# Two groups on the two partition halves with paired 64-row products, a sparse diagonal of the maxima, and GpSimd's style product first in its slot

## The reference

```python
styles = w @ (affine_w * gain).T + affine_b                       # one style per batch
y = clip(einsum(x * styles, weight) * dcoefs + bias, -256, 256)   # modulated linear
Q, K, V = X @ Wq, X @ Wk, X @ Wv          # X = y; 16 heads in 4 groups, key width 64
attn = softmax(Q K.T / 8)                 # 128 x 128 for each head
x = x + y + (attn @ V) @ Wpost
kx = modulated_linear(x)                  # 16 heads of 8 channels within one token
out = modulated_linear(softmax(kx kx.T / sqrt(8)) kx)
x = x + experts(out)                      # 8 experts, top 2, capacity rule
```

## Time and profile before

| | |
|---|---|
| Median of three runs | 663.79 us (662.43 to 665.09) |
| Profiled execution, own time | 664.89 us |
| Its span, first to last instruction | 663.1 us |
| TensorE, VectorE, ScalarE, GpSimd busy | 96%, 79%, 62%, 43% of the span |
| Mean granted clock of TensorE | 0.989 of full |

### The profile page before, as it was taken

One profiled execution on the slowest core, in us unless ns is written; L12 is line 12 of the kernel. 1 busy time (PEld: TensorE's weight loads), 2 busy tenths in 40 slices (PEclk: granted clock), 3 DMA queues, 4 the chain that ended last, 5 costly groups with the idle time before them and its releaser, 6 DMA issues. The chain is left out here.

```text
span 663.1 us, 15299 instructions
## 1 busy us (share of the span) xinstructions
PE 634.1 (96%) x4420; PEld 511.7 (77%) x4420; DVE 521.7 (79%) x1155; ACT 414.1 (62%) x823; POOL 288.1 (43%) x251
## 2 busy tenths in 40 slices
PE   8899999999999999999999999999999996899998
PEld 8687778787878787878787877778787786756765
DVE  6246888888888888888888888888888879767776
ACT  2776677767676777777777777777767531434443
POOL 5122555555555555555555555555555466000000
PEclk9999999999999999999999999999999997899999
DMA  7200000000000000000000000000000000000004
GB/s 245 47 1 1 1 2 1 0 0 0 0 0 0 0 0 0 0 0 0 0 0 0 0 0 0 0 0 0 0 0 1 2 1 1 0 0 0 1 0 127
DMA packets 9363, 7.18 MB, mean 11 GB/s; under 512 B 1088, under 2 KB 8832, under 8 KB 9216
## 3 DMA queue, kind: packets, MB, share of 16 engines
q1 hardware_dynamic: 9344, 6.94, 3.6%
HBM read 4.84 MB, written 2.10 MB: 10 GB/s over the span
## 5 line engine op out<-in xcount | busy, mean ns | idle before, releaser
L1087 POOL TENSOR_TENSOR pair<-kx 128x1152 f32<-128x1152 f32 x32 | 82.4, 2574 | 164.2 <-ACT kx L831 159.9
L611 PEld LDWEIGHTS bank_a<-v,prob 128*128 128x128 f32 x1024 | 127.0, 192 | 17.0 <-issue 15.8
L611 PE MATMUL bank_a<-v,prob 128*128 128x65 f32 x1024 | 131.8, 272 | 0.0
L603 PE MATMUL bank_t<-qT,k_one 128*128 128x512 f32 x256 | 130.7, 592 | 0.0
L295 DVE TENSOR_REDUCE row_max<-bank_s 128x4 f32<-128x512 f32 x128 | 87.3, 682 | 13.2 <-PE bank_s L594 8.9
L831 ACT ACTIVATE prob<-bank_t 128x512 f32<-128x512 f32 x128 | 76.4, 597 | 29.5 <-PE bank_t L603 26.5
L440 DVE CAST k<-k_one 64x512 bf16<-64x512 f32 x32 | 50.2, 1568 | 54.5 <-ACT k_one L831 54.5
L1067 POOL TENSOR_TENSOR mix_hi<-mix_hi 128x512 f32<-128x512 f32 (+2 forms) x96 | 80.2, 835 | 7.5
L1079 POOL TENSOR_TENSOR neg_diag<-neg_max,own_w 16x512 bf16<-16x512 f32 x32 | 36.3, 1135 | 96.2 <-ACT neg_max L831 83.5
L831 ACT ACTIVATE qT<-misc 64x512 f32<-64x512 f32 x128 | 75.6, 591 | 3.9 <-PE misc L618 1.6
L618 PEld LDWEIGHTS misc<-yT,wq_sb 128*128 128x128 f32 x512 | 64.5, 192 | 15.9 <-issue 14.9
(11 more groups left out here) (155 smaller groups left out, 1127.1 us busy)
## 6 DMA issues: line engine op xcount, KB each, us to landing
out<-acc_all SPq DMA_DIRECT2D x8, 256.0 KB, 2.3
x_all<-in_xT SPq DMA_DIRECT2D x1, 1024.0 KB, 9.6
w_sb<-in_w SPq DMA_DIRECT2D x2, 512.0 KB
x_all<-in_xT SPq DMA_DIRECT2D x1, 768.0 KB, 7.4
wq_sb<-in_wq SPq DMA_DIRECT2D x1, 512.0 KB, 6.1
wpost_sb<-in_wpost SPq DMA_DIRECT2D x1, 512.0 KB, 9.6
x_all<-in_xT SPq DMA_DIRECT2D x1, 256.0 KB, 3.1
b_rows<-in_b SPq DMA_DIRECT2D x16, 4.0 KB
```

The source lines that it names most:

```text
L603: mm(bank_t[g % 2][:, :, :], k_one[:, j, g, :], qT[:, j, HPG * g:HPG * (g + 1), :], start=False, stop=True).then_inc(s_t_mm, 1)
L611: last = mm(att_bank(g)[:, w, :], prob[:, g % 2, w, :], v1[:, j, g, :], start=(w == 0), stop=True, skip_group_check=True)
L1087: G.tensor_tensor(pair[:, :, :], bass.AP(kx2, jc * 2 * P, [[4 * P, P], [0, SHIFTS], [1, P]]), bass.AP(kx2, jc * 2 * P, [[4 * P, P], [MD, S ...
```

## The change

- `qT`, `q16`, `kT` and `k16` hold two groups at once: an even group on partitions 0 to 63, an odd one on 64 to 127. The columns of `wq` are put in another order on the host for it. `copy_q` is one copy of 128 partitions for each bank, `narrow_q` has half the columns, and the memsets of the unused halves go.
- `scores_t` takes a pair of groups: two bfloat16 products of 64 rows into `bank_t0` and `bank_t1`, then four float32 products of 64 rows and 256 columns that alternate between the halves.
- `row_max` becomes a bfloat16 tile of four blocks of 128 columns, in which only the places of a diagonal are written. Four small products with `ident16` into `bank_s` turn it, and one ScalarE copy with scale -1 makes `neg_diag`. GpSimd's instruction and `neg_max` go.
- `k16` and `v1` are made by ScalarE out of PSUM; VectorE's L440 goes.
- The order in a slot changes on each engine. In TensorE's, the second half of the queries comes before the maxima's product, `attend` 0 and 1 follow each other, and the style product of the batch after next stands in the middle and not at the end. VectorE makes `yT` after the first two groups. GpSimd makes `xs` first.

The core of the diff:

```diff
-                V.tensor_reduce(row_max[:, KEY + HPG * g:KEY + HPG * (g + 1)], bank_s[:, :, :], AX.X,
-                                ALU.max).then_inc(s_max, 1)
+                V.tensor_reduce(bass.AP(row_max, max_row(g), [[HPG * P, P], [P + 1, HPG]]).unsqueeze(2),
+                                bank_s[:, :, :], AX.X, ALU.max).then_inc(s_max, 1)
...
-                    V.tensor_copy(k16[0:KEY, ja, :, :], k_one[0:KEY, ja, :, :]).then_inc(s_k16, 1)
...
-                mm(bank_t[g % 2][:, :, :], g_rows[:, g, :], neg_diag[:, j, :, :], start=True, stop=False)
-                mm(bank_t[g % 2][:, :, :], k_one[:, j, g, :], qT[:, j, HPG * g:HPG * (g + 1), :],
-                   start=False, stop=True).then_inc(s_t_mm, 1)
+            def scores_t(s, j, p):
+                need(pe, s_prob, 4 * s + 2 * p)
+                pe.wait_ge(s_neg, n(s))
+                for half in range(2):
+                    rows = slice(KEY * half, KEY * (half + 1))
+                    mm(bank_t[half][:, :, :], g_rows[rows, 2 * p + half, :], neg_diag[rows, j, :, :],
+                       start=True, stop=True, skip_group_check=True)
+                for w in range(0, HPG, 2):
+                    for half in range(2):
+                        rows = slice(KEY * half, KEY * (half + 1))
+                        last = mm(bank_t[half][:, w:w + 2, :], kT[rows, j, p, :], qT[rows, j, p, w:w + 2, :],
+                                  start=False, stop=True, skip_group_check=True)
+                        if w == HPG - 2:
+                            last.then_inc(s_t_mm, 1)
...
-                    nc.tensor.transpose(misc[1][:, 0, :], row_max[:, :], ident[:, :]).then_inc(s_neg_mm, 1)
+                    for w in range(HPG):
+                        last = mm(bank_s[:, w, :], row_max[:, w, :], ident16[:, :],
+                                  start=(w == 0), stop=True, skip_group_check=True)
+                    last.then_inc(s_neg_mm, 1)
...
-                for par in range(2):
-                    f(qT[0:KEY, j, HEADS // 2 * half + par:HEADS // 2 * (half + 1):2, :],
-                      qkv_bank(b, ("q0", "q1")[half])[par * KEY:(par + 1) * KEY, :, :]).then_inc(s_q, 1)
+                f(qT[:, j, half, :, :], misc[half][:, :, :]).then_inc(s_q, 1)
...
-                    f(neg_max[KEY:KEY + HEADS, :], misc[1][KEY:KEY + HEADS, 0, :], scale=-1.0).then_inc(s_neg, 1)
+                    f(neg_diag[:, j, :, :], bank_s[:, :, :], scale=-1.0).then_inc(s_neg, 1)
...
+                    f(k16[:, ja, :, :], misc[0][:, 0:2, :]).then_inc(s_k16, 1)
...
-                    G.tensor_tensor(neg_diag[rows, j, :, :],
```

More of the change, by code:

```diff
@@ L88, in build @@
         yT = sb("yT", [P, P])
[L90 to L93, removed]
+        qT = sb("qT", [P, 2, PAIRS, HPG, P])
+        q16 = sb("q16", [P, 2, PAIRS, HPG, P], BF16)
+        kT = sb("kT", [P, 2, PAIRS, P])
+        k16 = sb("k16", [P, 2, PAIRS, P], BF16)
         v1 = sb("v1", [P, 2, GROUPS, KEY + 1])
-        row_max = sb("row_max", [P, P])
-        neg_max = sb("neg_max", [P, P])
+        row_max = sb("row_max", [P, HPG, P], BF16)
         prob = sb("prob", [P, 2, HPG, P])
@@ L467, in slot @@
                     V.tensor_scalar(yT[:, :], y_raw[:, :], CLAMP, -CLAMP, ALU.min, ALU.max).then_inc(s_yT, 1)
+                if A:
+                    group_max(a, 0)
+                if B:
+                    invert(s, 2)
+                    normalise(s, 2)
+                if A:
+                    group_max(a, 1)
+                if B:
+                    invert(s, 3)
+                    normalise(s, 3)
+                if A:
+                    group_max(a, 2)
             slots(dve, slot)
@@ L615, in queries @@
             def queries(b, half):
-                bank = qkv_bank(b, ("q0", "q1")[half])
+                bank = misc[half]
                 for c in range(4 * half, 4 * half + 4):
@@ L637, in gate_logits @@
                 pe.wait_ge(s_tok, tiles[-1] + 1)
+                if tiles[0] == EARLY[0]:
+                    pe.wait_ge(s_neg, BATCH)
                 for b in tiles:
@@ L659, in slot @@
                 if C:
-                    bank_free(pe, 1, s, "att0")
+                    if s_is(c, 0):
+                        pe.wait_ge(s_q, 2 * n(s))
+                    need(pe, s_kx2, c)
                     att_transpose(c, 0)
[L662 to L668, removed]
                 if s_is(s, -1):
@@ L694, in slot @@
                 if A:
-                    if not s_is(a, 0):
-                        bank_free(pe, 0, s, "q1")
-                    queries(a, 1)
+                    pe.wait_ge(s_q, 2 * a + 1)
+                    bank = misc[0]
+                    for i in range(2):
+                        mm(bank[:, i, :], wk_sb[:, i * P:(i + 1) * P], yT[:, :],
+                           start=(i == 0), stop=True, skip_group_check=True)
+                    mm(bank[:, 2:4, :].rearrange("p a f -> p (a f)"), yT[:, :], wv_sb[:, :], start=False,
+                       stop=True, skip_group_check=True).then_inc(s_kv_mm, 1)
                 if C:
-                    bank_free(pe, 1, s, "kx")
+                    if A:
+                        pe.wait_ge(s_q, 2 * a + 2)
                     pe.wait_ge(s_x1s, n(c))
@@ L704, in slot @@
                 if B:
-                    scores_t(s, j, 1)
+                    attend(s, j, 0)
+                if s_is(s, BATCH - 1):
+                    gate_logits(parts_early[1])
+                if B:
+                    attend(s, j, 1)
                 if C:
@@ L708, in slot @@
                     nc.tensor.transpose(misc[1][:, 0, :], kxT[:, :], ident[:, :]).then_inc(s_kxn_mm, 1)
[L709 to L712, removed]
-                if D:
-                    bank_free(pe, 2, s, "mix")
+                if has(a + 1):
+                    if A:
+                        pe.wait_ge(s_v, n(a))
+                        pe.wait_ge(s_k16, n(a))
+                    pe.wait_ge(s_xs, n(a + 1))
+                    mm(misc[0][:, 0, :], modw_sb[:, 0, :], xs[:, j, :], start=True, stop=True).then_inc(s_y_mm, 1)
+                if D:
+                    if C:
+                        pe.wait_ge(s_x1T, n(c))
+                    if s_is(s, BATCH + 1):
+                        keep_going(40)
+                    if s_is(s, BATCH + 2):
+                        keep_going(12)
+                    need(pe, s_mixT, d)
                     pe.wait_ge(s_mix, n(d))
@@ L719, in slot @@
                 if B:
[L720 to L741, removed]
+                    scores_t(s, j, 1)
                 if s_is(s, -1):
@@ L748, in slot @@
                     keep_going(3)
+                if late(s):
+                    keep_going(3)
+                if D:
+                    pe.wait_ge(s_mixT, n(d))
+                    if has(a + 1):
+                        pe.wait_ge(s_y_raw, n(a + 1))
+                    need(pe, s_tok, d)
+                    mm(misc[0][:, 0, :], modw_sb[:, 2, :], mixT[:, :], start=True, stop=True).then_inc(s_o_mm, 1)
                 if B:
-                    scores_t(s, j, 3)
+                    attend(s, j, 2)
                 if A:
@@ L922, in slot @@
                     exp_scores(s, 0)
+                    exp_scores(s, 1)
+                if A:
+                    act.wait_ge(s_kv_mm, n(a))
+                    need(act, s_t_mm, 4 * n(a - 2))
+                    f(kT[:, ja, :, :], misc[0][:, 0:2, :]).then_inc(s_k, 1)
                 if C:
@@ L975, in slot @@
                       bias=modb_sb[:, 0:1]).then_inc(s_y_raw, 1)
+                if D:
+                    act.wait_ge(s_mixT_mm, n(d))
+                    need(act, s_o_mm, n(d - 1))
+                    act.wait_ge(s_style, 3)
+                    f(mixT[:, :], misc[2][:, 0, :], scale=style[:, 2, bass.ds(d, 1)]).then_inc(s_mixT, 1)
+                if s_is(s, BATCH):
+                    copy_logits(EARLY, 6)
+                if not late(s):
+                    head_weights()
+                if B:
+                    exp_scores(s, 2)
+                    exp_scores(s, 3)
+                if D:
+                    act.wait_ge(s_o_mm, n(d))
+                    act.wait_ge(s_demod, 5)
+                    f(tok_all[:, col(d)], misc[0][:, 0, :], ACT.Identity, scale=demod[:, 2, bass.ds(d, 1)],
+                      bias=modb_sb[:, 2:3]).then_inc(s_tok, 1)
                 if s_is(s, BATCH + 2):
@@ L1055, in xs_of @@
                                     style[:, 0, bass.ds(b, 1)].to_broadcast([P, P]), ALU.mult).then_inc(s_xs, 1)
+                if isinstance(s, int) and s == -2:
+                    pool.wait_ge(s_ld_x0, 16)
+                if isinstance(s, int) and s + 2 == QUAD:
+                    pool.wait_ge(s_ld_x, 32)
+                if has(s + 2):
+                    xs_of(s + 2, j)
                 if D:
```

192 lines of the change are left out of this document (57 added, 135 removed).

## The result

The changed kernel takes 685.76 us in the median of four runs (681.67 to 687.82), the one before 664.3: a ratio of 1.031 (1.0285 to 1.0343). It is 3.1% slower where I forecast 6% faster. The profiled execution has a span of 679.9 us.

The account below looks back on a forecast made before the run. TensorE was taken to bound the kernel. A slot going from 16.36 to 15.12 us, times 31, gave 38 us, the start 2: 40 off 664.9 made 625, 624 for the median; own range 608 to 640, wide range 598 to 658.

Parts of the forecast that it names:

- the walk through the slot: All engines' steps from the first transposes to the next slot: 14.87 us plus 0.25 for five passages, against 16.36 before.
- the rival of both bounds at once: TensorE's pairs don't overlap and every passage costs a full drain: slot 17.08 us, 684 in all; chance 0.05.
- the passages to 64 rows: TensorE's changes between 128-row and 64-row products, five runs a slot: 0.05 us each, bounds nothing to 0.27.
- The overlap: A pair's float32 products on different partition halves run partly together on TensorE: 1.29 us a pair, bounds 1.08 to 2.15.
- The slot before: The kernel before's loop slot, taken as 16.36 us; less 15.12 it gave 1.24 a slot, 38 us over 31.
- The start: Before the first scores, which wait for `k16` until 20.37 us: 18.7 after the change, about 2 us less.
- the cast's wait: VectorE's cast L440 was held up by GpSimd's `pair`; the stall was to pass to `yT`, median near 1.4 us.
- `shifted` stayed ahead of `pair`: VectorE's `shifted` keeps 0.44 us before GpSimd's `pair`; rivals had it fall behind: nearly all slots 712 (0.08), every other 667 (0.05).
- `neg_diag` and ScalarE had cover: ScalarE makes `neg_diag` at 4.05 us of the slot, before TensorE's output product ends at 5.02: 0.9 us of cover.
- The rival in which `yT` isn't held up: VectorE's `yT` doesn't wait for GpSimd's `pair`: slot 14.42 us, 62 less, 602 in all; chance 0.15.
- The rival of no overlap: The halves' products on TensorE don't run together, `pair` 0.86 us later: slot 15.98, 650 in all; chance 0.13.
- my upper bound: Each of five passages on TensorE costs a drain of 0.27 us: slot 16.22, 658 in all; that rival's chance 0.12.

Follow-up runs that it names:

- the filled kernel: The changed kernel with three float32 products of ones between `attend` 2 and scores 1, where TensorE stands still: 645.34 us, 0.974 of the kernel before.
- the kernel with `yT` later: The changed kernel with `yT` behind `group_max` 0 on VectorE instead of in front of it: 628.71 us, ratio 0.948.
- the two kernels that freed it: The changed kernel with `y_raw` written to PSUM for `yT` to read, 632.2 us; and the changed kernel with `yT` behind `group_max` 0, 628.71 us.
- the same-rows run: The changed kernel with both products of a pair on rows 0 to 63, so the output is not the reference's: 693.34 us, a slot 16.69.
- the kernel before with one hole: The kernel before with one more wait, `attend` 2 waiting for `group_max` 1 of the next batch: 691.44 us, ratio 1.041.
- two holes: The kernel before with two more waits, ahead of `attend` 2 and `attend` 3: 770.2 us.

## Why the prediction was wrong

The step that failed is the walk through the slot ending in 15.12 us: I summed it at full clock and wrote "TensorE idles about 1 us a slot then" without asking what that does to the clock. What the runs showed in its place is a granted clock of 0.90 in the slots. Against the forecast (624) the median is 62 off, and it divides so (times by medians, slots and the start by the profiles):

- *The clock*, 40 us: 685.76 against 645.34 with the hole filled. It was in no rival. That the rival of both bounds at once had 684 is luck: the halves do overlap, and a passage doesn't cost what it took.
- *The slot at full clock*, 10 us: 15.45 (the filled kernel) against 15.12, times 31. Two errors in it. `pair` starts at 10.56 of the slot (334.69 less 324.13), not 9.97: TensorE comes to the transpose of `kxT` 0.23 later, the copy to `kx2` starts 0.18 later behind it (334.06), and GpSimd another 0.18 (0.25 after the copy, where I had 0.07). And the passages to 64 rows are dearer: the queries take 0.99 with scores behind them and 0.89 else, the scores 0.33 against 0.23, so 0.2 for a run of 64 rows and not 0.05. The overlap is better than I took it, 1.09 for the second pair and 1.19 for the first, not 1.29.
- *The slot before*, 8 us: I subtracted from 16.36, the longer of two kinds of slot in the loop, where the mean by the earlier trace rows is 16.09.
- *The start*, 3 us: the first product of the maxima stands at 26.2, 1.0 later than before, not 2 earlier. I did not look for the cause, and part of it may be chance: in two profiles of the kernel with `yT` later it stands at 25.0 and 23.1.

Together 61 of 62.

What held: the bound was TensorE's; the 64-row products of different halves overlap; `yT` took over the cast's wait behind `pair` (1504 ns, forecast about 1400) and sent it on to `group_max` 0 and scores 1; `shifted` stayed ahead of `pair`; `neg_diag` and ScalarE had cover. The rival in which `yT` isn't held up gave 602, and the two kernels that freed it took 629 and 632: right in kind, too far by the same errors in the slot. The rival of no overlap is refuted by the same-rows run, in which a slot takes 16.69 where that rival had 15.98: about what five dearer runs of 64 rows make (0.75). Of the Trainium skill's page TensorEngine Tiling (Array Packing), Key Properties, the first half (tiles work in parallel) agrees with the trace; for the second, a drain at each change of mode, the rows show about 0.1 us into and 0.1 out of a run of 64 rows, 0.2 together, where my upper bound was 0.27.

What caused the fall of the clock: a hole of 0.79 us alone does not do it (the kernel before with one hole), the overlap without the hole does it seldom or not at all (the two freed kernels; the filled one), neither of them doesn't (same rows), and holes alone do it when there are more of them (two holes). So in the changed kernel it is the saved streaming and the hole together; that the hole without overlap leaves the clock up was shown in the kernel before, not in the changed one. The Trainium skill's page TensorE: Matmul & The Clock Gate, What's actually happening, ties the clock to how busy TensorE has been recently. The runs agree in kind, but the profile's busy time doesn't put them in order: from 277 to 497 us TensorE is busy 203.34 at a clock of 1.00 with one hole in the kernel before, and 216.23 at 0.98 where `yT` reads PSUM. How the chip judges it was not tried.

## What to carry to other kernels

When a change takes work from a bounding engine and leaves it waiting, the time saved may be paid for in its clock. Before forecasting a gain on TensorE, ask whether what remains still fills it, and in the profile after it read the granted clock before anything else; filling a hole with idle products tells in one run how much the clock costs. A stall on a shared SBUF path moves to the next instruction of the same kind: look on which side of the critical instruction it stands, since a swap of two neighbours was worth 57 us here.

## What the runs showed of the hardware that I had not expected

- The granted clock fell to 0.50 with no standstill of TensorE longer than 0.82 us in the slot shown, and stood at 1.00 in the kernel before with one of 0.79.
- Float32 products on the two row halves overlap almost wholly, 0.86 us for eight instructions of 256 columns against 1.73 on the same rows (317.48 to 319.21), and mostly also when they are not issued in turns (1.41 a pair against 1.19).
- An instruction of VectorE that reads one SBUF source and took 0.23 us took up to 2.35 us beside GpSimd's `pair`, and never more than 0.29 with the same data in PSUM.
